# A vector product of the second layer's network, moved from the end of the first adjacency product into the first chunk's network stages

## The reference, cut to what matters

```
h = relu(conv(h, W2, b2));  x = x + (hin + h) * 0.5      # second convolution
h = relu(layernorm(x))
agg = segment_sum(edge_attr, dst)                        # 64 values for each node
h = concatenate([h, agg, u[0]], axis=1)                  # 128 + 64 + 64
h = leaky_relu(h @ w1 + b1)
h = leaky_relu(h @ w2 + b2)
x = x + h @ w3 + b3
```

## Time and profile before

| | us |
|---|---|
| median of 3 runs | 1178.48 (1177.75 to 1178.62) |
| the profiled execution, its own time | 1181.4 |
| its span | 1179.6 |
| TensorE busy | 1075.1 (91%) |
| VectorE busy | 721.8 (61%) |
| ScalarE busy | 534.0 (45%) |
| the last phase, from its first matmul | 751.83 to the end |

### The profile page before, as it was taken

One profiled execution on the slowest core, in us unless ns is written; L12 is line 12 of the kernel. 1 busy time (PEld: TensorE's weight loads), 2 busy tenths in 40 slices (PEclk: granted clock), 3 DMA queues, 4 the chain that ended last, 5 costly groups with the idle time before them and its releaser, 6 DMA issues. The chain is left out here.

```text
span 1179.6 us, 30059 instructions
## 1 busy us (share of the span) xinstructions
PE 1075.1 (91%) x9799; PEld 707.8 (60%) x9800; DVE 721.8 (61%) x1203; ACT 534.0 (45%) x1243; POOL 255.6 (22%) x184
## 2 busy tenths in 40 slices
PE   1999899866999999999999997599999999999995
PEld 1999889865666666666666654454444444444442
DVE  5558565539999999999999926422332323332232
ACT  1012345507888888888888844312121211212212
POOL 3445201535962322222332000000000000000000
PEclk9999899985999999999999998899999999999997
DMA  6999799700566666666555569977887777777710
GB/s 219 304 372 320 247 302 303 237 17 17 192 207 199 198 198 198 198 198 198 190 188 186 184 196 285 311 221 253 263 247 236 225 229 227 237 224 243 240 36 20
DMA packets 225240, 252.62 MB, mean 214 GB/s; under 512 B 13898, under 2 KB 192063, under 8 KB 225048
## 3 DMA queue, kind: packets, MB, share of 16 engines
q1 hardware_dynamic: 110372, 144.56, 38.4%
q10 hardware_dynamic: 109828, 96.49, 25.3%
q0 software_dynamic: 4976, 10.71, 2.8%
HBM read 161.74 MB, written 90.00 MB: 213 GB/s over the span
## 5 line engine op out<-in xcount | busy, mean ns | idle before, releaser
L974 ACT CAST adj_all<-win_p 128x392 f32 x784 | 342.6, 497 | 52.1 <-PE win_p L1023 33.8
L1023 PEld LDWEIGHTS win_p<-adj_all,st 128*128 128x128 f16 x3136 | 215.4, 101 | 145.2 <-ACT adj_all L974 29.5
L1023 PE MATMUL win_p<-adj_all,st 128*128 128x98 f16 x3136 | 256.8, 213 | 23.0 <-ACT adj_all L974 16.3
L924 DVE TENSOR_TENSOR st<-iota_lo,code 128x2048 f16 x196 | 243.2, 1241 | 15.6 <-ACT code L963 8.1
L1038 PE MATMUL dense_p<-adj_all,g_hi 128*128 128x448 f16 x686 | 241.0, 351 | 1.2 <-DVE total L935 0.9
L1038 PE MATMUL dense_p<-adj_all,g_lo 128*128 128x448 f16 x686 | 241.6, 352 | 0.0
L1632 PE MATMUL dense_p_b<-adj_all,g_hi 128*128 128x512 f16 (+1 forms) x637 | 231.9, 372 | 3.7 <-issue 3.4
L1632 PE MATMUL dense_p_b<-adj_all,g_lo 128*128 128x512 f16 (+1 forms) x637 | 231.7, 371 | 0.0
L754 PE MATMUL agg_p<-ahot,arows 128*64 128x64 f32 x3240 | 203.3, 226 | 13.6 <-DVE ahot L465 7.6
L754 PEld LDWEIGHTS agg_p<-ahot,arows 128*64 128x64 f32 x3240 | 198.2, 141 | 19.0 <-issue 17.9
L924 DVE TENSOR_TENSOR adj_all<-iota_mv,code 128x1568 f16 x196 | 193.2, 986 | 0.0
(11 more groups left out here) (204 smaller groups left out, 810.4 us busy)
## 6 DMA issues: line engine op xcount, KB each, us to landing
adj_d<-adj_all ACTq DMA_DIRECT2D x14, 5488.0 KB, 19.5
adj_all<-adj_d SPq DMA_DIRECT2D x11, 6272.0 KB, 23.5
arows<-in_edge_attr_dram SPq DMA_DIRECT2D x45, 960.0 KB
adj_all<-adj_d ACTq DMA_DIRECT2D x1, 6272.0 KB, 35.2
disb<-dis_d SPq DMA_DIRECT2D x24, 256.0 KB, 5.7
arows<-in_edge_attr_dram SPq DMA_DIRECT2D x9, 640.0 KB
h<-in_x_dram ACTq DMA_DIRECT2D x4, 768.0 KB
hT_d<-hT ACTq DMA_DIRECT2D x12, 256.0 KB, 6.2
```

Source lines behind the costliest of these rows:

```text
L924: ins = nc.vector.tensor_tensor(hot[:, bass.ds((b * BG + j) % 2, 1), u, :, :] .rearrange("p a w (n t) -> p (a w) n t", t=2), iota[:, :].re ...
L974: nc.scalar.copy(adj[:, bass.ds(b % 2, 1), :, bass.ds(j * GN + k * WN, WN)] .rearrange("p b h d -> p (b h) d"), win_p[:, k % 4, 0:WP * MV] ...
L1023: ins = nc.tensor.matmul(win_p[:, k % 4, 0:WP * MV] .rearrange("p (h c t) -> p h c t", c=WP, t=PN)[:, :, c, :], st[:, odd, k // UW, pair, ...
```

## The change

`u_product` leaves the first multiply. The wait for the weights that stood at its head (and VectorE's and ScalarE's at the head of their programs) goes to where a weight is first used: ahead of chunk (0, 0)'s `linear` on TensorE and ahead of its first activation on ScalarE. The product itself stands at the head of chunk (0, 0)'s `turn_back`; VectorE's sum stands behind the `shift` of that chunk, and ScalarE waits for `s_c1` ahead of the first use of `c1_sb`. The stages of chunk (0, 0) get a table of their own, FIRST_AFTER, by which they stand later in `multiply(0, 1)`: `linear` after k = 14, where it stood after k = 5.

```
+            FIRST_AFTER = (14, 18, 30, 33, 38, 43, 46)
...
                         nc.vector.memset(xt[:, 0, 0, :], 0.0).then_inc(s_pad, 1)
-                        dve.wait_ge(s_w, 16 * 11)
-                        dve.wait_ge(s_uc, 1)
-                        nc.vector.tensor_tensor(c1_sb[:, :], c1_sb[:, :], lin_p[:, 0:M1], ALU.add).then_inc(s_c1, 1)
...
+                            if not two_before(i) and h == 0:
+                                dve.wait_ge(s_w, 16 * 11)
+                                dve.wait_ge(s_uc, 1)
+                                nc.vector.tensor_tensor(c1_sb[:, :], c1_sb[:, :], lin_p[:, 0:M1], ALU.add
+                                                        ).then_inc(s_c1, 1)
                             dve.wait_ge(tpb_done, c + 1)
...
                         act.wait_ge(s_out, 16 * len(BATCH))
-                        act.wait_ge(s_w, 16 * 11)
-                        act.wait_ge(s_c1, 1)
...
+                            first = not two_before(i) and h == 0
+                            if first:
+                                act.wait_ge(s_w, 16 * 11)
                             gate(act, lin_done, c + 1)
...
                             ins.then_inc(hl_ready, 1)
+                            if first:
+                                act.wait_ge(s_c1, 1)
...
                     def u_product():
-                        pe.wait_ge(s_w, 16 * 11)
...
                         def linear():
+                            if first:
+                                pe.wait_ge(s_w, 16 * 11)
                             pe.wait_ge(mixed, c + 3)
...
                         def turn_back():
+                            if first:
+                                u_product()
                             pe.wait_ge(hl_ready, c + 1)
...
-                            multiply(0, 0, 1, [lambda: None] * (len(AFTER) - 1) + [u_product])
-                            multiply(0, 1, NT, stages(0, 0, 1))
+                            multiply(0, 0, 1, [])
+                            multiply(0, 1, NT, stages(0, 0, 1), FIRST_AFTER)
```

More of the change, by code:

```diff
@@ L1622, in stages, with multiply @@
                         return [linear, turn_to_nodes, turn_back, mlp1, mlp2, mlp3, turn_y]
-                    def multiply(i, h, n, between):
+                    def multiply(i, h, n, between, behind=AFTER):
                         c = i * 2 + h
@@ L1634, in multiply @@
                                                        stop=(k == HI - 1 and g is g_lo))
-                            if k in AFTER and AFTER.index(k) < len(between):
-                                between[AFTER.index(k)]()
+                            if between and k in behind:
+                                between[behind.index(k)]()
                         ins.then_inc(dense_done, 1)
@@ L1647, in program @@
                         else:
-                            u_product()
                             for stage in stages(0, 0, 1) + stages(0, 1, NT):
```

## The result

| | before | after |
|---|---|---|
| median | 1178.55 us | 1172.15 us |
| lowest to highest of 6 runs | 1177.75 to 1180.84 | 1170.14 to 1174.17 |
| ratio, 95% interval | | 0.9935, 0.9918 to 0.9951 |
| profiled execution, its span | 1181.4, 1179.6 | 1172.31, 1170.6 |

The change is faster. The forecast was 1172.5, a ratio of 0.9949, and that lies in the interval. The ratio itself, taken to the median that the prediction started from (1178.48), gives 1170.8 us, a gain of 7.7 instead of the 5.95 forecast, and this is 0.4 us outside the range. The interval is wide: it stands for gains of 5.8 to 9.7 us, and the two medians of the table differ by 6.4 only, a ratio of 0.9946.

A forecast was written before the change was run, and what follows sets the result against it. TensorE bounds the adjacency product; the third multiply starts at the later of 784.9 (TensorE alone) and 787.0 (load landing), so 793.00 - 787.05 = 5.95 us earlier: 1178.48 - 5.95 = 1172.5 us, range 1171.2 to 1175.2.

The forecast's parts named there:

- What bounds, and the stall: Adjacency product: TensorE is the bound; its 6.12 us idle for the last weight load, ahead of `u_product`, goes away.
- TensorE alone: Second multiply: without waiting for loads, TensorE would end it at 784.9 (759.55 + 24.22 + 1.1), range 784.1 to 785.1.
- The moved waits: Chunk (0, 0)'s stages in the second multiply: waits at `linear`, VectorE's sum and ScalarE's `s_c1` cost nothing.
- What is late next: Third multiply's adjacency load on SyncE: issued at 764.0, flight 23.0, landing at 787.0; TensorE waits about 2.1 us.
- the ring order: Third multiply's load: bias vectors' descriptors stand ahead in the same rings, flight nearer 24.7, time 1.7 us above forecast.
- The size: Third multiply starts 793.00 - 787.05 = 5.95 us earlier, giving 1172.5 us; some 0.5 allowed for medians of other runs.
- The distance behind it: From the third multiply to the end of the span: unchanged at 386.6 us.
- The clock in the new wait: Wait ahead of the third multiply: TensorE loses its upper clock, up to 2.3 us, time 1174.8; chance 0.09.
- SyncE's stall at the loop: SyncE stalls entering its loop, as much as 3.38 us; landing at 790.4, gain 2.6, time 1175.9; chance 0.08.
- The load that doesn't bind: Third multiply's load is there before TensorE: gain 8.1 us, time 1170.4, needs a flight of 20.9; chance 0.05.
- the wait that stays: TensorE waits for the weights inside the second multiply nearly as long as before: under 2 us won, 1177; chance 0.03.
- the slow flight: Third multiply's load meets other traffic, flies 35.2 us and lands at 799.2: slower, 1184.7; chance 0.03.

## Why the prediction was right in its steps and short in its size

**What bounds, and the stall.** Right. The 6.12 us went, TensorE goes straight on into the second multiply, and its data were there.

**TensorE alone.** Forecast 784.9, which is 33.07 behind the phase's start; measured 782.99 - 1.81 - 748.11 = 33.07. Counted by starts it is a little less: the last matmul ahead of the wait started at 780.79, the next could have at 781.01, which is 32.9. The agreement hides misses that nearly cancel. The second multiply began 6.78 and not 7.72 behind the start, as the clock came up early in this trace, which is luck; and `linear` waited 0.55 for the weights where nothing was forecast, because TensorE was early. `u_product` with its hand-over took 0.93 (770.26 to 771.19); forecast 1.1.

**The moved waits.** Right but for the 0.55 above: VectorE's sum, the `shift` ahead of it and ScalarE's wait cost nothing but the 0.33 counted in `u_product`.

**What is late next.** Right, and the run with four extra loads and that with the small loads on ScalarE show it: the third multiply moves one for one with SyncE's issue when that is later, and is no longer set by the load when it is 2.2 us earlier. Issue forecast 12.2 behind the start, measured 12.2 to 12.4. Flight forecast 23.0, measured 22.2 to 22.4. Wait forecast 2.1, measured 1.81, and the third multiply 34.88 against 35.22. The 1.7 us that the prediction had set beside the forecast by the ring order of the Trainium skill, page "DMA: Bandwidth & Descriptors", section "Queues, rings and completion order", did not show: with the small vectors directly ahead of it the load flew 22.2 to 22.6 us (six traces), while it took 21.2 to 22.7 when it was issued 2.6 to 5.0 us behind the load ahead of it in the queue (seven traces).

**The size.** This is the step that failed: the sum's one term for the gain, 793.00 - 787.05 = 5.95, and the 0.5 us that the range allows for everything outside it. The 793.00 was taken from one trace of before, as if 41.17 were the kernel's value. Three traces of it give 41.17, 41.57 and 42.06, mean 41.60: the end of the stall varies (13.77 to 14.51), and the time until the clock is back varies by 1.1. Against 34.85 the change is worth 6.75 at its place, 0.8 more than forecast; 0.4 of that is the shorter flight (22.2 to 22.4 for the forecast 23.0) and 0.4 the trace of before. The change took out not only a wait but a cost behind it that varies from run to run. These 0.8 us are less than half of the 1.75 by which the forecast fell short; the other part follows under what stays open.

**The distance behind it.** Right from the third multiply to the last `linear` (357.8 and 357.9). The tail is longer in the three traces of after (29.3 to 29.7) than in those of before (28.8 to 29.0), by 0.7 us; the clock changes there between its two levels.

**What stays open.** 6.75 - 0.7 is 6.1, and the gain by the ratios was 7.7 and 7.8. Either interval alone (5.8 to 9.7 us) still holds 6.1, so the difference may be noise, though nearly the same ratio came twice. If there is a difference of 1.6, it lies ahead of the phase, where the prediction's sum put nothing. In the traces of before the windows begin at 265.8 to 269.7, in those of after at 262.0 to 263.4; in the eight kernels with other edits at 262.9 to 267.4, with no order that follows the edits (262.9 and 263.5 for two that leave the product where it was). The traces of before overstate this, as all three are of executions longer than the median: taking the mean distances of the table from the medians, I estimate the beginning at 263.4 to 264.5 for before and 262.4 to 263.0 for after. No instruction ahead of that point is changed by any of the kernels. Between the first traces of before and after the difference grows in steps from some 48 us on, in the aggregation of edges, which is fed by DMA. Whether it is chance between executions or hangs on the built program, these runs don't tell. The prediction's range gave 0.5 us for it and should have given 1.5 to 2, as single runs of before reach from 1175.8 to 1188.4.

**The rivals.** The clock in the new wait (the one that the prediction had set beside the Trainium skill's page "TensorE: Matmul & The Clock Gate", section "HAM oscillation — how this bites in real kernels"): not with 1.81 us here, but with 2.42 to 3.96 in four experiments; a chance of 0.09 was low for a forecast wait of 2.1. The waits for DMA in that section of the Trainium skill are given as some 3 to 5 us, so they were no measure for one of 2.1. The 3.96 us here agree with it; no run here has a wait between 1.81 and 2.42 in such a place. SyncE's stall at the loop: the issue came 0.92 behind the last weight, so there is none of size. The load that doesn't bind, the wait that stays and the slow flight did not come; but flights of 21.2 and 21.3 us in two of the experiments are below the 22.7 that the prediction had taken for the least.

## What to carry to other kernels

A wait can be moved off the bounding engine by placing its consumer later, but the gain is capped by what comes next on the queue that fed it: here an in-order queue of eleven small DMA issues, 7 us long, held a large load of another buffer. Compute when the next load can be issued, and try whether an idle engine's queue can take some of the issues; here that brought the third multiply 1.25 us forward in one trace, and nothing that the timed runs resolve. Measure a stall from several executions before its removal is priced: the slow clock behind it is part of it and varies.

## What the runs showed of the hardware

- Idle time of TensorE behind dense matmuls cost nothing at 1.2 and 1.81 us. At 2.42, 2.89 and 3.01 us the clock fell after work had been taken up again (2.3, 1.2 and 0.9 us behind it), and at 3.96 us during the idle time; at 3.96 that was worth 2.4 us. Behind the 2.42 and 2.89 stand the product's short matmuls and another 0.33 us of waiting, behind the 3.01 dense work soon again, so the first two are not the price of the idle time alone. An idle time of 2.35 us stands in the tail of before, where the window shows 1.00; that row alone had made the wait look safe, but the clock fell there too, 1.7 us behind the return to sparse work:

```profile
1150.80:1152.00 1.20, 1.13 (x2) 0.30 (x2) 0.00 (x0) 0.00 (x0) 0.00 (x0) 1.00 0.38 113
1152.00:1153.50 1.50, 0.00 (x0) 0.00 (x0) 0.69 (x1) 0.69 (x1) 0.00 (x0) 0.67 0.00 0
```

- The clock came back between 4.6 and 5.5 us behind the end of the stall in the three traces of before, and between 2.8 and 5.6 us behind the first matmul in those of after, with the same code.
- A vector of 1 KB or less took 2.4 to 3.0 us to land when little else was under way, 5.1 to 5.8 beside a large load, and 4.6 to 5.5 beside four loads of 256 KB on another engine's queue.
- The load of 6272 KB for the third multiply flew 21.2 to 22.7 us in thirteen traces, and 23.5 in the one where it was issued directly behind four loads of 256 KB.
